# Two plain attentions with the maxima row outside the ring of PSUM banks, and a shared expert that takes no gates

## The reference

```python
x = x + attention0(layernorm(x))   # 16 heads of 8, rotary, no mask, softmax over 1024 keys
x = x + ffn0(layernorm(x))
x = x + attention1(layernorm(x))   # 16 heads of 8, with norm and biases, softmax over 1024 keys
x = x + ffn1(layernorm(x))         # relative attention, then 32 experts, top 4 of a sigmoid router

# ffn0: one shared expert and 7 routed ones, 128 -> 352 -> 128
def expert(h, g, u, d): return einsum('...i,hi->...h', silu(h @ g.T) * (h @ u.T), d)
out = expert(x, sg, su, sd)                     # shared: no gate
probs = softmax(x @ wr.T + rb)
scores, idx = top_k(probs, 2); scores = scores / scores.sum(-1)
for e in range(7): out = out + w[..., e] * expert(x, rg[e], ru[e], rd[e])
```

## Time and profile before

| | us |
|---|---|
| median of 3 runs (lowest, highest) | 2145.89 (2145.6, 2148.17) |
| the profiled execution | 2154.38 |
| its span, first to last instruction | 2152.2 |
| attention(0), first scores to last values | 48.2 to 400 |
| experts0, first product to last | 446 to 656 |
| attention(1) | 703.6 to 1056 |
| busy share PE, DVE, ACT, POOL | 93%, 66%, 56%, 24% |
| mean granted clock of TensorE | 0.944 |

### The profile page before, as it was taken

One profiled execution on the slowest core, in us unless ns is written; L12 is line 12 of the kernel. 1 busy time (PEld: TensorE's weight loads), 2 busy tenths in 40 slices (PEclk: granted clock), 3 DMA queues, 4 the chain that ended last, 5 costly groups with the idle time before them and its releaser, 6 DMA issues. The chain is left out here.

```text
span 2152.2 us, 43028 instructions
## 1 busy us (share of the span) xinstructions
PE 2002.8 (93%) x13792; PEld 1204.8 (56%) x13792; DVE 1415.1 (66%) x1857; ACT 1198.3 (56%) x2297; POOL 511.2 (24%) x495
## 2 busy tenths in 40 slices
PE   5999999779996899999768999999999999986998
PEld 2344444457774344444346666666666666664887
DVE  6899999356656899999566455455455545435776
ACT  2688888446662488888523444444444444443554
POOL 2000000048883000000122222222222222102664
PEclk8799999789997699999779999999999999997999
DMA  8444543121102544444161112111221112013564
GB/s 271 122 111 116 124 113 92 50 85 61 60 20 83 160 111 118 123 112 111 57 178 44 47 46 66 48 46 45 54 57 48 46 45 63 12 31 140 216 218 149
DMA packets 90287, 198.95 MB, mean 92 GB/s; under 512 B 19888, under 2 KB 49328, under 8 KB 84784
## 3 DMA queue, kind: packets, MB, share of 16 engines
q1 hardware_dynamic: 90224, 198.15, 32.2%
HBM read 163.47 MB, written 36.18 MB: 93 GB/s over the span
## 5 line engine op out<-in xcount | busy, mean ns | idle before, releaser
L1157 DVE TENSOR_REDUCE M<-PS 128x1 f32<-128x1024 f32 x512 | 599.4, 1220 | 59.3 <-PE PS L610 59.3
L1428 ACT ACTIVATE PR<-PS 128x512 f32<-128x512 f32 x1024 | 535.9, 590 | 115.6 <-PE PS L630 114.7
L1467 ACT ACTIVATE PR<-PS 128x512 f32<-128x512 f32 x512 | 306.1, 598 | 377.4 <-PE PS L739 373.5
L1178 DVE TENSOR_REDUCE M<-PS 128x1 f32<-128x1024 f32 x256 | 311.9, 1222 | 219.5 <-PE PS L725 212.4
L630 PE MATMUL PS<-Qs_r,Ks_r 32*128 32x512 f32 x1024 | 380.9, 512 | 1.7 <-ACT PR L1428 1.4
L640 PE MATMUL PS<-PR,Va 128*32 128x256 f32 x4096 | 326.4, 404 | 0.0
L610 PE MATMUL PS<-Ks_r,Qs_r 32*128 32x512 f32 x1024 | 268.1, 521 | 16.9 <-DVE M L1157 10.9
L610 PEld LDWEIGHTS PS<-Ks_r,Qs_r 32*128 32x128 f32 x1024 | 99.6, 191 | 198.1 <-issue 127.1
L630 PEld LDWEIGHTS PS<-Qs_r,Ks_r 32*128 32x128 f32 x1024 | 153.1, 187 | 93.1 <-ACT PR L1428 69.2
L1173 DVE TENSOR_TENSOR rt<-PS,rel 128x512 f32<-128x512 f32 x128 | 88.5, 691 | 155.4 <-PE PS L697 153.9
L1601 POOL TENSOR_TENSOR Va<-Vt,nil 128x64 f32<-128x64 f32 x96 | 27.9, 294 | 610.6 <-PE PS L640 601.0
(11 more groups left out here) (196 smaller groups left out, 3096.1 us busy)
## 6 DMA issues: line engine op xcount, KB each, us to landing
Qs_r<-q_stack SPq DMA_DIRECT2D x384, 128.0 KB, 2.6
Ks_r<-k_stack SPq DMA_DIRECT2D x384, 128.0 KB, 3.1
Qs<-g_dram SPq DMA_DIRECT2D x30, 1024.0 KB, 4.8
o_dram<-Ob SPq DMA_DIRECT2D x96, 128.0 KB, 2.5
Ks<-g_dram SPq DMA_DIRECT2D x10, 1024.0 KB, 4.9
q_stack<-hl SPq DMA_DIRECT2D x18, 256.0 KB, 3.2
k_stack<-hl SPq DMA_DIRECT2D x18, 256.0 KB, 3.9
q_stack<-PR_r SPq DMA_DIRECT2D x18, 256.0 KB, 3.3
```

The costliest lines, as they stand in the source:

```text
L1157: e.tensor_reduce(M[:, s, qt:qt + 1], PS[:, 2 + 2 * (qt % 2):4 + 2 * (qt % 2), :] .rearrange("p a b -> p (a b)"), AX.X, ALU.max, negate=Tr ...
L1178: e.tensor_reduce(M[:, s, qt:qt + 1], PS[:, bk:bk + 2, :].rearrange("p a b -> p (a b)"), AX.X, ALU.max, negate=True).then_inc(max_done, 1)
L1428: e.activation(PR[:, kt % 4, qh * GW:(qh + 1) * GW], bank(RING[(x if x < 4 else x + 1) % 3]), ACT.Exp, scale=SCALE).then_inc(exp_done, 1)
L1467: e.activation(PR[:, kt % 4, qh * GW:(qh + 1) * GW], bank(TURN[kt % 2][qh]), ACT.Exp)\
```

## The change

It has two parts. In the plain attentions the maxima row moves to columns 256 to 383 of bank 6, beside the sums of `values`. The ring holds only turned tiles, x + turn modulo 3, where turn is the head's number modulo 3; so the code of a head repeats after 12 heads, and the loop has 12, two times, with heads 25 to 31 written out behind it. The values run three steps behind the tiles: steps 0 to 2 have blocks 5 to 7 of head n - 1, steps 3 to 7 blocks 0 to 4 of head n. In step 2 TensorE waits for the copy of the maxima row before block 7. ScalarE has `max_copy` after exponential 3 and `evacuate` after exponential 4.

```diff
-    def max_row(n, s):
+    def max_row(n, s, alone=False):
 
         e.wait_ge(max_done, 2 + 8 * (HB + n) + 8)
-        e.wait_ge(exp_done, 16 * (HB + n - 1) + 4)
-        e.matmul(PS[0:QT, RING[1], 0:P], M[:, s, :], ident[:], start=True, stop=True).then_inc(mt_done, 1)
-
-    def turned(n, s, x):
-
-        if x < 3:
-            e.wait_ge(exp_done, 16 * (HB + n) + (1, 2, 2)[x])
-        elif x == 6:
-            e.wait_ge(mt_copied, HB + n + (1 if isinstance(n, int) and n == NH - 1 else 2))
-        else:
-            e.wait_ge(exp_done, 2 + 16 * (HB + n) + (x - 1 if x in (4, 5) else x - 2))
+        e.matmul(PS[0:QT, 6, 256:256 + P], M[:, s, :], ident[:], start=alone, stop=True,
+                 skip_group_check=True).then_inc(mt_done, 1)
+
+    def turned(n, s, x, turn):
+
+        e.wait_ge(exp_done, 16 * (HB + n) + x)
         rows_ = slice(x % 2 * KR, (x % 2 + 1) * KR)
         kt, qh = x // 2, x % 2
-        e.matmul(bank(RING[(x if x < 4 else x + 1) % 3]), Ks_r[rows_, s, kt * P:(kt + 1) * P],
+        e.matmul(bank(RING[(x + turn) % 3]), Ks_r[rows_, s, kt * P:(kt + 1) * P],
                  Qs_r[rows_, s, qh * GW:(qh + 1) * GW], start=True, stop=True).then_inc(st_done, 1)
...
-            turned(n, s, 2 * kt)
-            turned(n, s, 2 * kt + 1)
-            if kt < 2 and not first:
-                values(n - 1, (s - 1) % SLOTS, QT - 2 + kt)
+            turned(n, s, 2 * kt, turn)
+            turned(n, s, 2 * kt + 1, turn)
+            if kt == 2 and rows_next:
+                e.wait_ge(mt_copied, HB + n + 2)
+            if kt >= 3:
+                values(n, s, kt - 3)
+            elif not first:
+                values(n - 1, (s - 1) % SLOTS, QT - 3 + kt)
             if kt == 1 and rows_next:
-                max_row(n + 1, (s + 1) % SLOTS)
-            if kt == 3:
-                values(n, s, 0)
-            if kt >= 3:
-                values(n, s, kt - 2)
+                max_row(n + 1, (s + 1) % SLOTS, alone=first)
...
             if n == 1 and qt == 1:
-                e.wait_ge(max_done, 2 + 8 * HB + 8)
-                e.matmul(PS[0:QT, RING[1], 0:P], M[:, 0, :], ident[:], start=True, stop=True)\
-                    .then_inc(mt_done, 1)
+                max_row(0, 0, alone=True)
     e.wait_ge(mt_copied, HB + 1)
-    position(0, 0, 0, first=True)
-    with e.Fori(0, NH // SLOTS - 1) as i:
-        for s in range(1, SLOTS + 1):
-            position(SLOTS * i + s, i + s // SLOTS, s % SLOTS)
-    for s in range(1, SLOTS):
-        position(NH - SLOTS + s, NH // SLOTS - 1, s, ahead=s < 2, rows_next=s < 3)
-    for kt in range(QT - 2, QT):
+    position(0, 0, 0, 0, first=True)
+    with e.Fori(0, 2) as i:
+        for s in range(1, 3 * SLOTS + 1):
+            position(3 * SLOTS * i + s, 3 * i + s // SLOTS, s % SLOTS, s % 3)
+    for n in range(6 * SLOTS + 1, NH):
+        position(n, n // SLOTS, n % SLOTS, n % 3, ahead=n < NH - 2, rows_next=n < NH - 1)
+    for kt in range(QT - 3, QT):
         values(NH - 1, SLOTS - 1, kt)
...
 
     def max_copy(n, s):
         e.wait_ge(mt_done, HB + n + 1)
-        e.activation(MT[:, s, :], PS[0:QT, RING[1], 0:P], ACT.Copy).then_inc(mt_copied, 1)
-
-    def position(n, s, pairs, first=False, rows_next=True):
+        e.activation(MT[:, s, :], PS[0:QT, 6, 256:256 + P], ACT.Copy).then_inc(mt_copied, 1)
+
+    def position(n, s, pairs, turn, first=False, rows_next=True):
         for x in range(16):
             kt, qh = x // 2, x % 2
-            if x == 4:
-                if not first:
-                    evacuate(n - 1, (s - 1) % SLOTS, pairs)
-                if rows_next:
-                    max_copy(n + 1, (s + 1) % SLOTS)
+            if x == 4 and rows_next:
+                max_copy(n + 1, (s + 1) % SLOTS)
+            if x == 5 and not first:
+                evacuate(n - 1, (s - 1) % SLOTS, pairs)
             e.wait_ge(st_done, 1 + 16 * (HB + n) + x + 1)
             if qh == 0:
                 e.wait_ge(pv_done, 8 * (HB + n) + kt + 1)
-            e.activation(PR[:, kt % 4, qh * GW:(qh + 1) * GW], bank(RING[(x if x < 4 else x + 1) % 3]),
+            e.activation(PR[:, kt % 4, qh * GW:(qh + 1) * GW], bank(RING[(x + turn) % 3]),
                          ACT.Exp, scale=SCALE).then_inc(exp_done, 1)
 
...
-    with e.Fori(0, NH // SLOTS - 1) as i:
-        for s in range(1, SLOTS + 1):
-            position(SLOTS * i + s, s % SLOTS, 2 * i + (s - 1) // 2)
-    for s in range(1, SLOTS):
-        position(NH - SLOTS + s, s, NH // 2 - 2 + (s - 1) // 2, rows_next=s < 3)
+    position(0, 0, 0, 0, first=True)
+    with e.Fori(0, 2) as i:
+        for s in range(1, 3 * SLOTS + 1):
+            position(3 * SLOTS * i + s, s % SLOTS, 6 * i + (s - 1) // 2, s % 3)
+    for n in range(6 * SLOTS + 1, NH):
+        position(n, n % SLOTS, (n - 1) // 2, n % 3, rows_next=n < NH - 1)
     evacuate(NH - 1, 3, NH // 2 - 1)
```

```diff
+        hl0, hl0_r = two("hl", [P, 2, 2, GW])
+        hls = [hl0_r, PR_r[:, 0:2, :].rearrange("p a (b t) -> p a b t", b=2)]
...
-        GTs = BIG[0:NE1, 4096:4096 + TT * P]
+        route_mem = hl0[:].rearrange("p a b t -> p (a b t)")
+        lg, lg2, gate = (route_mem[:, o:o + TT * w].rearrange("p (t x) -> p t x", t=TT)
+             for o, w in ((0, NE1 + 8), (TT * (NE1 + 8), NE1 + 8), (2 * TT * (NE1 + 8), NE1)))
+        GTs = [atn[0:NE1, 0, :], atn[0:NE1, 1, :], xn[0:NE1].rearrange("p t d -> p (t d)"), BIG[0:NE1, 15 * GW:16 * GW]]
...
-def experts(k):
-    slots = 2 + k
-    gates_out(k)
-    for x in range(slots):
+def experts0():
+
+    e.wait_ge(w0_ok, 1)
+    load_expert(0, 2, 0)
+    gates_out(0)
+    for x in range(1, 3):
+        load_gate(x, x % 2)
+    for x in range(1, NE0 - 2):
+        e.wait_ge(w0_ok, x + 1)
+        load_expert(0, x + 2, x % 2)
+        e.wait_ge(xw_ok, NG * x)
+        load_gate(x + 2, x % 2)
+
```

TensorE:

```diff
 def experts0():
 
-    zero_acc(0)
+    zero_acc(0, range(4, 7))
     x_parts = (XTh, XTl)
+
+    def gate_rows(tg, g):
+
+        if tg != 2:
+            return
+        e.wait_ge(gate_ok, 1)
+        e.wait_ge(gt_ok_a, g)
+        gates(g, 7)
 
...
-    def up(place, par, tg, c, k):
+    def up(place, par, tg, c, k, shared):
         lo, w = FCH[c]
-        h = [xwp[r][:, tg % 2, :] for r in range(2)] if k else \
+        h = [xwp[r][:, tg % 2, :] for r in range(2)] if k and not shared else \
             [x_parts[r][:, tg * GW:(tg + 1) * GW] for r in range(2)]
...
+        up(0, par, tg, 0, 0, first)
         e.wait_ge(h_ok, count(3 * v - 1))
-        up(1, par, tg, 1, 0)
+        up(1, par, tg, 1, 0, first)
         par2, tg2 = (par, tg - 1) if tg else (1 - par, NG - 1)
         before = not (first and tg == 0)
+        if first:
+            gate_rows(tg, 0)
         if before:
             down(v - 1, par2, tg2, 0)
         e.wait_ge(sg_ok, count(3 * v))
-        e.wait_ge(xlo_ok, v + 1)
-        up(2, par, tg, 0, 1)
+        if not first:
+            e.wait_ge(xlo_ok, v + 1 - NG)
+        up(2, par, tg, 0, 1, first)
+        if first:
+            gate_rows(tg, 1)
         if before:
             down(v - 1, par2, tg2, 1)
         e.wait_ge(h_ok, count(3 * v))
-        up(3, par, tg, 1, 1)
+        up(3, par, tg, 1, 1, first)
         e.wait_ge(sg_ok, 3 * v + 1)
-        up(4, par, tg, 2, 0)
+        if first:
...
             down(v - 1, par2, tg2, 2)
         e.wait_ge(sg_ok, 3 * v + 2)
-        up(5, par, tg, 2, 1)
+        up(5, par, tg, 2, 1, first)
+        if first:
+            gate_rows(tg, 3)
 
     for tg in range(NG):
         unit(0, 0, tg, True, False)
+    e.wait_ge(gt_ok_a, NG)
+    zero_acc(0, range(7, 8))
```

VectorE:

```diff
-    if a2 is None:
-        route(f)
+    if f == 1:
+        route_clear()
+    if f == 4:
+        route_clear()
+        route_logits(4)
+        route_top(4)
+        route_gates(4)
...
 
 def experts0():
+    route_logits(1)
     zero_acc()
...
 
         if tg == 0:
             e.wait_ge(gb_in[par], 16 * (k + 1))
-        e.wait_ge(xlo_ok, count(v - 1))
...
+    def products(x, par, tg, last):
         v = NG * x + tg
-        if not (last and tg == NG - 1):
-            if tg < NG - 1:
-                gated(v + 1, x, par, tg + 1, k)
-            else:
-                gated(v + 1, x + 1, 1 - par, 0, k)
...
                 weights(x + 1, 1 - par)
 
+    def unit(x, par, tg, k, k_next, last):
+        v = NG * x + tg
+        if tg < NG - 1:
+            gated(v + 1, par, tg + 1, k)
+        elif not last:
+            gated(v + 1, 1 - par, 0, k_next)
+        products(x, par, tg, last)
+
     weights(0, 0)
-    gated(0, 0, 0, 0, 0)
-    for tg in range(NG):
-        unit(0, 0, tg, 0, False)
+    route_top(1)
+    products(0, 0, 0, False)
+    route_gates(1)
+    for tg in range(1, NG):
+        products(0, 0, tg, False)
+    gated(NG, 1, 0, 0)
     with own.loop(NE0 // 2 - 1, 2) as i:
```

(15 more changed lines are left out.)

## The result

| | before | after |
|---|---|---|
| median of 4 runs, us (lowest to highest) | 2147.03 (2145.6 to 2152.06) | 2118.99 (2117.84 to 2121.73) |
| profiled execution, us | 2154.38 | 2119.04 |
| mean granted clock | 0.944 | 0.946 |

The account below looks back on a forecast made before the run. TensorE, VectorE and ScalarE were close to full, none the plain bound, VectorE waiting for TensorE. Profiled 2154.4 less 23 (attentions) less 12.5 (experts) gave 2118.9, less 8.5 to the median 2110 us; range 2090 to 2132.

Parts of the forecast that it names:

- Heads in the loop: Plain attentions: a head takes 9.77 us for 10.19, 0.42 less; 58 heads give 24.4 us.
- steps 2 and 3: Head of plain attention: TensorE waits for the maxima row's copy before block 7, then for the evacuation before block 0.
- Step 4: Head of plain attention: exponentials 5 and 6 late, tile 9 waits until 5.48 us, next step at 6.48.
- the same walk: Head of plain attention: step times added up from measured hops between engines; it retraced the old 10.19 us period.
- Rival 2: Plain attentions stay at 10.19 us a head, the new chain of waits taking the gain: 2133 us; chance 0.17.
- The jump: End of the 12-head loop body, once in each attention: possibly 4.5 us, left out of the sum.
- rival 3: Jump back of the 12-head body in each attention costs 4.5 us, 9 us more: 2119 us; chance 0.13.
- rival 1: Plain attentions: the ring runs through, ScalarE's copies hide, VectorE's 9.39 us ends the head: 2086 us; chance 0.09.
- The tails: End of each plain attention: three values blocks for two at a low clock, 1.0 us each, 2.0 us charged.
- The profile against the median: Whole kernel: profiled execution 2154.4 falls to 2118.9; 8.5 us above the median, so 2110 us.
- Experts: Router and shared expert: expert 1 begins 13.3 us earlier, 0.8 taken off for late products: 12.5 us, from 8 to 15.
- rival 4: Long loop body fetched while it runs, TensorE standing still 2.67 us in each head: 2276 us; chance 0.05.

Follow-up runs that it names:

- e7: Kernel before with values three steps behind and evacuation after exponential 4, maxima row still in the ring, bodies of 4 heads: 2167.48 us, a head 10.42 to 10.53.
- e8: Kernel after with values where they stood before and the row's copy right ahead of the evacuation, maxima row in bank 6: 2120.77 us, a head 9.83.
- e9: Kernel before, order of work untouched, with loop bodies of 12 heads run twice instead of bodies of 4: 2161.32 us.
- e10: Kernel before, order of work untouched, with loop bodies of 8 heads run three times instead of bodies of 4: 2171.49 us.
- e2: Kernel after with the old attention, so only router and shared expert changed: 2132.56 us, ratio 0.992 to the kernel before.
- e4: Kernel before with its loops of 4 heads written out on TensorE and ScalarE, old order: 2128.28 us, ratio 0.991, a head 9.96.
- e11: e3 with the rest of the router ahead of unit 0's products, gate transposes in unit 1, first gated product earlier on VectorE: 2087.57 us, ratio 0.970.
- e3: Kernel after with the loops of 12 heads written out on TensorE and ScalarE, same order: 2088.87 us, ratio 0.971 to the kernel before.
- e12: e3 with VectorE's loop over the row maxima written out as well: 2086.11 us, ratio 0.971, a head 9.39.

## Why the prediction came out as it did

**Heads in the loop: right.** 9.77 walked, 9.75 measured, and the waits stand in steps 2 and 3 where they were put. Single hops were off by 0.07 to 0.13, in both directions, and the total came out as well as it did because they cancel: block 7 to evacuation 0.79 for 0.86, copy to block 7 0.38 for 0.31, evacuation to TensorE 0.53 for 0.40. Step 4, too, took 0.11 less than foreseen. Still, the same walk gave the two half orders of e7 and e8 to 0.1 us. Rival 2 (the chain eats the gain) fell.

**The jump: the step that failed.** It stood among the rivals at 0.13 and as nothing in the sum. The earlier trace rows show jumps that cost nothing, but with bodies of 4 heads; the text said itself that no row decides for longer ones. Stall and low clock came, 10.1 and 3.9 us for two times 4.5 foreseen; e9 and e10 show them with the old order. This term has 14 us, more than the whole 9 between forecast and time; that the time is rival 3's 2119 is luck in the number, since its two jumps cost 5 us more than it gave them and other terms made up for that.

**The straight heads: not seen.** The last heads run at 9.40, rival 1's pace, about 5 in each attention, 2 x 5 x 0.35 = 3.5 us of gain that the sum lacks. Before held a trace of it, its one head with scores behind the loop took 10.11 for 10.19, and the prediction makes nothing of it.

**The tails: the wrong sign.** Three values blocks at the end were charged 2.0 us on the ground of a low clock there; they gained 0.7 in all. After: last copy to first `atn` 18.24 us; old order at full clock 18.60 (e2, e4, e9, e10). The low clock was of that execution, not of the code; a tail can still meet it (23.22 and 19.51 us for the two tails of e7). Together the last two terms return some 6 of the 14 us.

**The profile against the median: the agreement is luck.** 35.5 us were predicted on the profiled execution and 35.3 came, but not as the steps add up: 8 us of them are the two slow tails of before. Taking off 8.5 for the median assumed that the execution after would lie as far above its median; it lay on it (2119.04 and 2118.99), and against the 25 later runs of before the offset was 4.6. The other differences by stage are of the size that one code shows from run to run: over the kernels shown here front(1) took 27.0 to 30.4 us and the rest of the program 1093 to 1102. The heads at the low clock, from the first scores to the third copy, took 31.8 us in attention(0) of the kernel after (4.0 less than before), and 32.4 to 35.9 in all the other attentions.

**Experts: right in size.** 13.3 us foreseen up to expert 1, 13.26 measured; 12.5 and 11.7 in all. Zeroing 4.3 us, as foreseen (4.3). Unit 0 took 4.6 us for 4.2. Unit 2 took 9.3 us for 8.1, since it also holds waits for the copy of a piece of the gates (0.57 at 439.60) and for GpSimd's low part (0.37 at 437.35); unit 3 and bank 7 took 6.8 for 7.2. The stall ahead of the gated product was foreseen with 0.9 us and came with 0.78. The gates were as late as foreseen, and VectorE's place for `gated` was equally late (451.3 and 451.50), which the prediction didn't have. e11 moves both and takes 0.9 of the 1.3 us away.

**Long straight code (rival 4): fell.** e3 has 32 heads in a row on both engines and no gap.

## To carry to other kernels

Where engines hand each other small tiles, read the pace in a loop and in the same code written out, if the kernel has both: the difference is the price of the loop's form, here 0.35 us of 9.75 a head, most of it on ScalarE. A change that lengthens a loop body has to be priced with its jump, by a body of that length and not by the short one before it; the trace's packets of instructions tell whether the engine still holds the body. And before a sum is set against a profiled execution, look at the granted clock of its quiet stretches: a tail at half clock need not be the code's.

## What the runs showed of the hardware

- A jump back costs nothing visible with bodies of 4 heads, for which no instructions are brought in, and 3.2 to 3.9 us of standstill on TensorE with 8 or 12, whatever the order of work; no longer for 12 than for 8. With the loop on ScalarE alone the two jumps took 5.4 and 1.8 us.
- Behind such a standstill TensorE's granted clock was 0.50 (1.2 GHz) for up to 20 us in some places and low for under 5 in others, with the same code and nearly the same gap (3.70 and 3.23 us in the kernel after). That makes 10.1 and 3.9 us out of the two stalls.
- A hop in a loop, where the wait's value comes from a register, took about 0.08 us longer than in straight code (0.38 and 0.30, 0.79 and 0.71), and it counts only where the wait ends last: on VectorE it cost nothing (e12), and in the relative attention, bound by TensorE, a head in the loop and the one with scores behind it both take 24.3 us (kernel before).
